# A long convolution stage and a transformer layer on one core: angles counted in turns, attention values with 512 moving columns, weights' low parts a window later in a third buffer

## The reference

```python
dt = jnp.exp(log_dt)
dt_Lambda = dt[:, None, 0] * Lambda[None, :, 0] + 1j * (dt[:, None, 1] * Lambda[None, :, 1])
...
Wc = Wc * num * _reciprocal(den * Lam, EPS)
P = dt_Lambda[..., None] * pos - P_max[..., None]
K = jnp.einsum('chn,hnl->chl', Wc, jnp.exp(P))
return K.real.astype(jnp.float32)
```

```python
attn = jax.nn.softmax(scores, axis=-1)
ctx = jnp.einsum('bhqk,bhkd->bhqd', attn, v_h)
ctx = ctx.transpose(0, 2, 1, 3).reshape(b, t, D_OUT)
return ctx @ Wo
...
h = _L0_tok_ref(L0_tok_log_dt, L0_tok_Lambda, x, 1024)
h = h + _L0_attn_ref(_layernorm(h, axis=-1), ...)
h = h + _L0_ffn_ref(_layernorm(h, axis=-1), ...)
```

## Time and profile before

| | us |
|---|---|
| median of 3 runs | 2391.71 (2391.33 to 2392.13) |
| the profiled execution, whole | 2390.53 |
| its span, first to last instruction | 2388.7 |
| one chunk of the first stage (122.44 to 149.07) | 26.63 |
| the layer stage's first instruction | 262.1 |

### The profile page before, as it was taken

One profiled execution on the slowest core, in us unless ns is written; L12 is line 12 of the kernel. 1 busy time (PEld: TensorE's weight loads), 2 busy tenths in 40 slices (PEclk: granted clock), 3 DMA queues, 4 the chain that ended last, 5 costly groups with the idle time before them and its releaser, 6 DMA issues.

```text
span 2388.7 us, 58825 instructions
## 1 busy us (share of the span) xinstructions
PE 2276.2 (95%) x18704; PEld 1246.2 (52%) x18704; DVE 1908.7 (80%) x7797; ACT 1836.2 (77%) x6269; POOL 1708.1 (72%) x1529
## 2 busy tenths in 40 slices
PE   2999689999999999999999999999999999999986
PEld 2777345555555555555555555555555555555543
DVE  8999578888788788888788878888888878888864
ACT  5998388777877777878777787777787777778773
POOL 1444187877777777777787777777777777777772
PEclk9999899999999999999999999999999999999997
DMA  2888599999999999999999999999999999999984
GB/s 77 263 252 240 135 172 186 187 186 191 189 185 194 188 183 193 191 187 185 191 184 190 192 190 186 189 193 177 192 191 187 187 193 190 180 196 186 184 170 100
DMA packets 1201602, 443.65 MB, mean 186 GB/s; under 512 B 1151622, under 2 KB 1153926, under 8 KB 1201292
## 3 DMA queue, kind: packets, MB, share of 16 engines
q1 hardware_dynamic: 1201284, 439.89, 91.5%
q10 hardware_dynamic: 8, 0.01, 0.0%
HBM read 87.40 MB, written 67.11 MB: 65 GB/s over the span
## 4 chain that ended last, share of the span: by engine, by line
PE 83%; ACT 2%; POOL 1%; DMA 1%; DVE 1%; issue 1%; POOLq 0%; DVEq 0%; ACTq 0%
PE pc L907 13%; PE pb L907 13%; PE pa L907 13%; PE s_ps L920 5%; PE pb L893 4%; PE pb L895 4%; PE pb L894 4%; PE pa L893 4%; PE pa L894 4%; PE pa L895 4%; PE pv_ps L935 4%; PE pd L893 2%; PE pd L895 1%; PE pd L894 1%; DMA pt<-p 1%; ACT pr L1059 1%
## 5 line engine op out<-in xcount | busy, mean ns | idle before, releaser
L1059 ACT ACTIVATE pr<-pr,smin 128x128 f32<-128x128 f32 x2048 | 793.5, 388 | 235.9 <-DVE smin L1205 235.7
L1425 POOL TENSOR_TENSOR pr<-pr,rinv 128x512 f32<-128x512 f32 x512 | 577.0, 1137 | 424.2 <-DVE rinv L1213 413.5
L1205 DVE CUSTOM_DVE_ANT_0 pr<-s_ps,cst 128x128 f32<-128x128 f32 x2048 | 468.7, 286 | 180.2 <-PE s_ps L920 95.7
L1433 POOL TENSOR_TENSOR p<-pr,p 128x512 f16<-128x512 f32 x512 | 590.1, 1158 | 23.9 <-ACT p L1069 13.0
L1069 ACT ACTIVATE p<-pr 128x512 f16<-128x512 f32 x512 | 319.0, 623 | 181.0 <-POOL pr L1425 153.4
L1059 ACT ACTIVATION_READ_ACCUMULATOR pr<-pr,smin 128x1 f32 x2048 | 382.1, 187 | 0.0
L907 PE MATMUL pa<-wkv_hi,xt 128*128 128x512 f16 x1024 | 326.3, 380 | 14.8 <-DMA xt<-xs 14.8
L907 PE MATMUL pb<-wq_hi,xt 128*128 128x512 f16 x1024 | 326.6, 380 | 0.0
L907 PE MATMUL pc<-wq_hi,xt 128*128 128x512 f16 x1024 | 315.0, 379 | 0.0
L642 PE MATMUL hps<-z,xw 128*128 128x256 f32 x848 | 193.7, 388 | 62.1 <-POOL xw L348 42.2
L642 PEld LDWEIGHTS hps<-z,xw 128*128 128x128 f32 x848 | 162.4, 194 | 92.9 <-POOL xw L348 50.5
(11 more groups left out here) (188 smaller groups left out, 4896.2 us busy)
## 6 DMA issues: line engine op xcount, KB each, us to landing
h<-rows SPq DMA_DIRECT2D x128, 256.0 KB, 3.5
h_res<-h SPq DMA_DIRECT2D x64, 512.0 KB, 4.5
out<-rows SPq DMA_DIRECT2D x64, 512.0 KB, 3.2
h_ln<-h SPq DMA_DIRECT2D x63, 512.0 KB, 4.2
pt<-p SPq DMA_TRANSPOSE x512, 3.8
xa<-x SPq DMA_DIRECT2D x16, 256.0 KB, 4.1
xb<-x SPq DMA_DIRECT2D x32, 128.0 KB, 3.8
wst<-wq SPq DMA_DIRECT2D x8, 512.0 KB, 5.7
```

What stands on the lines that cost most here:

```text
L1059: last = A.activation(p, p, ACT.Exp, bias=smin[g % 2][:, j:j + 1], scale=-1.0, accum_out=rsum[g % 2][:, j:j + 1])
L1205: V.tensor_tensor_reduce(pr[g % 2][:, cols], s_ps[g % 2][:, cols], mask, 1.0, 3e38, ALU.add, ALU.min, smin[g % 2][:, j:j + 1]).then_inc(ma ...
L1425: nc.gpsimd.tensor_tensor(p3, p3, rinv[g % 2][:, :].unsqueeze(2).broadcast_to([P, HG, P]), ALU.mult).then_inc(p_norm, 1)
L1433: nc.gpsimd.tensor_tensor(p[:, HG * P:], pr[g % 2][:, :], p[:, 0:HG * P], ALU.subtract).then_inc(pl_done, 1)
```

## The change

- Angles are counted in turns instead of radians: the rate `zi` is multiplied with 1/(2 pi) once at the start, and the whole turns are taken out with one pass of two operations (add a large number, subtract it) and one subtraction. The factor 2 pi goes into the sines' `scale`. `half` becomes twice the squared sine (`scale` of the square), so that `tables` is one pass, (half - 1) times expo, with the sign changed; `digits` is the same and the sign is taken up in the weights' last steps.
- `ON_ACT` is 3 in even windows and 2 in odd ones: in odd windows DVE makes two tokens of `xw` instead of one.
- `pi` has two buffers: DVE waits for the add two windows back instead of the one before.
- `wst` has three buffers, low parts are made one window later than in the list, and POOL's table steps no longer wait for low parts.
- `values` takes the four heads of a group as one moving operand of 512 columns, and four groups go to the four strips. The rows of `wo` are put into the matching order when inputs are laid out, before the kernel runs.

```diff
-ON_ACT = 3
+ON_ACT = (3, 2)
...
-                    if n >= 2:
-                        sp.wait_ge(w_lo, n - 1)
+                    if n >= WR:
+                        sp.wait_ge(w_lo, n - WR + 1)
...
-                    while loaded < len(PIECES) and PIECES[loaded - 2][0] <= w:
+                    while loaded < len(PIECES) and PIECES[loaded - WR][0] + LOW_LATER <= w + 1:
                         load_weight(loaded)
...
-                        lows = sum(piece[0] < w - 1 for piece in PIECES)
-                        if at in (0, 2, 3) and lows:
-                            pool.wait_ge(w_lo, lows)
...
-                    V.tensor_scalar(turns[:, :, :], theta[:, :, :], INV_2PI, MAGIC, ALU.mult, ALU.add).then_inc(tab_v, 1)
+                    V.tensor_scalar(turns[:, :, :], theta[:, :, :], MAGIC, MAGIC,
+                                    ALU.add, ALU.subtract).then_inc(tab_v, 1)
                     dve.wait_ge(tab_v, TV * k + 1)
-                    V.tensor_scalar(turns[:, :, :], turns[:, :, :], MAGIC, None, ALU.subtract).then_inc(tab_v, 1)
...
-                    V.tensor_scalar(theta[:, :, :], theta[:, :, :], PI_SAFE, -PI_SAFE,
-                                    ALU.min, ALU.max).then_inc(tab_v, 1)
+                    V.tensor_tensor(theta[:, :, :], theta[:, :, :], turns[:, :, :], ALU.subtract).then_inc(tab_v, 1)
...
-                    V.tensor_scalar(half[:, :, :], half[:, :, :], -2.0, 1.0, ALU.mult, ALU.add).then_inc(tab_v, 1)
...
-                    V.tensor_tensor(tab[k % 2][:, :, 0, :], expo[:, k * TC:k * TC + TC, :], half[:, :, :],
-                                    ALU.mult).then_inc(tab_v, 1)
+                    V.scalar_tensor_tensor(tab[k % 2][:, :, 0, :], half[:, :, :], 1.0,
+                                           expo[:, k * TC:k * TC + TC, :], ALU.subtract, ALU.mult).then_inc(tab_v, 1)
...
-                    if w >= 1:
-                        dve.wait_ge(xw_done, w)
+                    if w >= 2:
+                        dve.wait_ge(xw_done, w - 1)
...
                     for n, piece in enumerate(PIECES):
-                        if piece[0] == w:
+                        if piece[0] + LOW_LATER == w:
                             weight_lo(n)
+                weight_lo(len(PIECES) - 1)
...
-                        to = slice(P * (g % 4), P * (g % 4) + P)
-                        for n, (v, lo) in enumerate(((v_hi[odd], 0), (v_lo[odd], 0), (v_hi[odd], HG))):
-                            for j in range(HG):
-                                last = pe.matmul(pv_ps[j * HD:(j + 1) * HD, to], v[:, g * HD:(g + 1) * HD],
-                                                 pt[g % RP][:, lo + j, :], start=(n == 0), stop=(n == 2))
+                    for n, (v, lo) in enumerate(((v_hi[odd], 0), (v_lo[odd], 0), (v_hi[odd], HG))):
+                        for g in range(4 * m, 4 * m + 4):
+                            strip = slice(HD * (g % 4), HD * (g % 4) + HD)
+                            last = pe.matmul(pv_ps[strip, :], v[:, g * HD:(g + 1) * HD],
+                                             pt[g % RP][:, lo:lo + HG, :], start=(n == 0), stop=(n == 2))
```

More of the change, by code:

```diff
@@ L150, in s4_stage @@
         cst = W["cst"]
-        re_row, im_row, neg_re_row, row_sign = (cst[:, c:c + 1] for c in (C_RE, C_IM, C_NRE, C_SIGN))
+        re_row, im_row, row_sign = (cst[:, c:c + 1] for c in (C_RE, C_IM, C_SIGN))
         z = [sb(f"z{i}", [P, 4, QROW]) for i in range(ZR)]
@@ L156, in s4_stage @@
         xw = [sb(f"xw{i}", [P, WIN, TOPS, NB]) for i in range(XWR)]
-        pi = sb("pi", [P, WIN, TOPS, NB])
+        pi = [sb(f"pi{i}", [P, WIN, TOPS, NB]) for i in range(2)]
         expo = sb("expo", [P, T, NPOS])
@@ L162, in s4_stage @@
         hout = [W[f"rows{i}"] for i in range(HR)]
-        wst = [sb(f"wst{i}", [P, KC * AW]) for i in range(2)]
+        wst = [sb(f"wst{i}", [P, KC * AW]) for i in range(WR)]
         top_r = sb("top_r", [P, TOPS, T])
@@ L212, in s4_stage @@
         x_in = [sem(f"x_in{i}") for i in range(XR)]
-        w_in = [sem(f"w_in{i}") for i in range(2)]
+        w_in = [sem(f"w_in{i}") for i in range(WR)]
         w_hi = sem("w_hi")
@@ L244, in loads_until @@
         def loads_until(n):
-            return 16 * sum(PIECES[i][4] for i in range(n % 2, n + 1, 2))
+            return 16 * sum(PIECES[i][4] for i in range(n % WR, n + 1, WR))
         def weight(name, k):
@@ L375, in sines @@
                 def sines(k):
-                    act.wait_ge(tab_v, TV * k + 5)
-                    A.activation(half[:, :, :], theta[:, :, :], ACT.Sin, scale=0.5).then_inc(tab_a, 1)
+                    act.wait_ge(tab_v, TV * k + 2)
+                    A.activation(half[:, :, :], theta[:, :, :], ACT.Sin, scale=0.5 * TURN).then_inc(tab_a, 1)
                     act.wait_ge(tab_a, TA * k + 1)
-                    A.activation(theta[:, :, :], theta[:, :, :], ACT.Sin).then_inc(tab_a, 1)
-                    A.activation(half[:, :, :], half[:, :, :], ACT.Square).then_inc(tab_a, 1)
+                    A.activation(theta[:, :, :], theta[:, :, :], ACT.Sin, scale=TURN).then_inc(tab_a, 1)
+                    A.activation(half[:, :, :], half[:, :, :], ACT.Square, scale=ROOT_2).then_inc(tab_a, 1)
                 def products(w, e):
@@ L409, in _ @@
                 act.wait_ge(pre_v, V_F)
-                A.activation(sy, pf, ACT.Sin).then_inc(pre_a, 1)
-                A.activation(hy, pf, ACT.Sin, scale=0.5).then_inc(pre_a, 1)
+                A.activation(sy, pf, ACT.Sin, scale=TURN).then_inc(pre_a, 1)
+                A.activation(hy, pf, ACT.Sin, scale=0.5 * TURN).then_inc(pre_a, 1)
                 sines(0)
@@ L420, in _ @@
                 for w in range(LEAD):
-                    for e in range(ON_ACT):
+                    for e in range(ON_ACT[w % 2]):
                         products(w, e)
@@ L427, in _ @@
                     for e in range(WIN):
-                        if e < ON_ACT and w + LEAD < WINDOWS:
+                        if w + LEAD < WINDOWS and e < ON_ACT[(w + LEAD) % 2]:
                             products(w + LEAD, e)
@@ L551, in _ @@
                 step(V.tensor_tensor(yi, *lengthened(zi), ALU.mult))
-                step(V.tensor_scalar(pk, yi, INV_2PI, MAGIC, ALU.mult, ALU.add))
-                step(V.tensor_scalar(pk, pk, MAGIC, None, ALU.subtract))
-                step(V.scalar_tensor_tensor(pf, pk, -TWO_PI_HI, yi, ALU.mult, ALU.add))
-                step(V.scalar_tensor_tensor(pf, pk, -TWO_PI_LO, pf, ALU.mult, ALU.add))
-                step(V.tensor_scalar(pf, pf, PI_SAFE, -PI_SAFE, ALU.min, ALU.max))
+                step(V.tensor_scalar(pk, yi, MAGIC, MAGIC, ALU.add, ALU.subtract))
+                step(V.tensor_tensor(pf, yi, pk, ALU.subtract))
                 assert steps[0] == V_F
```

66 lines of the change are left out of this document (31 added, 35 removed).

## The result

The changed kernel takes 2370.78 us (median of 4 runs, 2369.04 to 2371.53), the one before 2391.52 us beside it on the same chip: 20.7 us less, a ratio of 0.9915 with a 95% interval of 0.9898 to 0.9932. The profiled execution took 2371.53, its span is 2369.1.

What follows compares the result with a forecast made beforehand. DVE was taken to bound the first stage (26.63 us a chunk, PE's floor 24.3), PE the layer stage. Gains of 15.3 and 1.7 us make 17: 2390.53 becomes 2374 profiled, 2375 median; range 2370 to 2380 (50%).

Steps and rivals of the forecast that it cites:

- The table pass, its place and its price: First stage, DVE's pass making `tab`: begins 14.38 us into the chunk, waits for POOL's late add, plus 2.1 us per chunk.
- The waits for ACT: First stage, DVE's two waits for ACT's high parts go when low parts come a window later: minus 1.54 us per chunk.
- The start: First stage ahead of the chunks: shorter angle passes and one table pass gone, minus 4.1 us in all.
- Chunk 0: First chunk: 1.2 us as the others, `pi` 0.4, and `wkv_lo` 0.6 moved into the next chunk: minus 2.2 us.
- Chunks 1 to 6: First stage, middle chunks: 25.4 us each instead of 26.63, minus 7.4 us together.
- Chunk 7: Last chunk: ACT wait of 1.63 us goes, `wo_lo` moves behind the last `z`, `wkv_lo` and longer `xw` enter: minus 1.6.
- POOL against the low parts: First stage: POOL's passes become free as DVE starts `wo_lo` and `wq_lo`; DVE wins, 0; otherwise plus 2.1 us per chunk.
- Rival 2: First stage: POOL's passes get in ahead of DVE's low parts, chunks of 27.5 us, 2387 us in all; 14%.
- SP's stores: First stage: h0 stores stand behind weight loads that wait 4 to 5 us; counted 0, at worst 1 us per chunk.
- Rival 1: First stage: DVE wins the race at `tab` and PE sets the pace, chunks of 24.3 us, 2367 us in all; 25%.
- The layer stage: Values step in three rounds of 512 columns, minus 2.7 us; waits for transposes at the end, plus 1: minus 1.7.
- rival 3: Values step: four strips do not stream together at 512 columns, about 2620 us (5%), or in part, 2396 us (3%).

Runs made afterwards that it cites:

- sines early: Changed kernel with ACT's sines for the next chunk moved from the start of a chunk's second window to its first window, behind the second eviction: 2356.84 us.
- add first: Changed kernel with POOL's order turned round in the window of `table_i`, the add ahead of `table_i`: 2364.96 us.
- three products: Changed kernel with three tokens of products on ACT in every window, `ON_ACT = (3, 3)`, as before the change: 2370.45 us.
- one `pi`: Changed kernel with one buffer of imaginary products instead of two: 2370.23 us.
- POOL's waits: Changed kernel with POOL's waits for the low parts of the weights put back: 2370.81 us.

## Why the prediction held, point by point

- **The table pass, its place and its price: right.** Forecast 14.38 us into the chunk, the sine's end 12.95, the add 14.3 to 16.65; measured 14.71 (14.37 in chunks 3 and 6), 12.95, and 14.27 to 16.63. The pass took 2.47 us, and the chunk 25.29 where 25.4 stood. That the meeting was the cause, and not DVE's sum, is shown by sines early and add first, which move work without taking any from DVE, and by three products, which takes 0.54 us from DVE and gains nothing. The changed kernel's own chunks say it too: where the second sine ends 12.95 or 12.96 us in (chunks 1, 3, 4 and 6), the chunk lasts 25.28 to 25.30, though chunk 1 has 1.28 us more of low parts; where it ends at 13.15 (chunk 2), 25.49, and at 13.86 (chunk 5), 26.03.
- **The waits for ACT: right that they go with late low parts**, and these carry most of the gain. The prediction took the angles' 1.64, the tables' 0.64 and the waits' 1.54 as one sum. As a sum it is right (23.35 for 23.37, with early sines), but its terms are not independent: without the late low parts the first two are worth nothing in a chunk.
- **The start: right**, PE's first matmul at 38.18 for 42.22, 4.04 us.
- **Chunk 0: too high, mostly by PE's clock.** Forecast 2.2 us, measured 0.5 (the sixth `pi` 69.16 to 64.62, less the 4.04). After 38 us without a matmul PE's records start 0.427 us apart, the rate of the lower clock level (1.2 GHz), and then 0.216; the rise came 6.0 us after the first matmul in this execution and 3.5 in the one before. The windows from 41 to 44 us of this kernel and of the one with one `pi`, where it came after 2.7 us (the clock column has no entry this early and prints 1.00):
```profile
41.00:44.00 3.00, 3.00 (x9) 2.37 (x8) 3.00 (x3) 1.54 (x5) 1.13 (x1) 1.00 0.00 0
```
```profile
41.00:44.00 3.00, 3.00 (x15) 2.65 (x14) 3.00 (x2) 2.15 (x6) 1.62 (x1) 1.00 0.00 0
```
Evictions wait for PE and the sines for evictions, hence DVE's 1.80 us. With one `pi` and with three products (3.0 us) chunk 0 gains 2.0 us by the same sum, as forecast, although the low part is as long there; with POOL's waits (5.7 us), 0.7. What set the moment is not shown.
- **Chunks 1 to 6: right**, 7.15 for 7.4 (228.97 to 217.28, less the 4.54 ahead). **Chunk 7: too low**, 2.98 for 1.6; 0.7 of it lies behind PE's last matmul, and no run takes it apart. The two misses cancel, by luck: 14.67 in all for 15.
- **POOL against the low parts: right**, DVE's low parts beside POOL's small passes are 1.21 to 1.22, and POOL's passes give way. (The two long `wq_lo`, 3.38 and 3.37 in chunks 0 and 5, wait for the add.) Rival 2 did not come.
- **SP's stores: counted 0, at worst 1 us per chunk; they cost about 0.9 in all.** SP stands up to 2.3 us before a load of weights (4 to 5 were forecast), and ACT's evictions wait 20.0 us for stores of h0. In most chunks that is over before the sines are due. In chunk 5 it is not: ACT waits 2.73 us, has two evictions to catch up, and makes the second sine 0.91 us later than in chunk 4; DVE's pass then comes ahead of the add, and the low part waits.
```profile
176.62 1.08 ACT L399 ACTIVATE rows<-hps 128x512 f32<-128x512 f32 x2 [2.73 <-DMA h<-rows]
...
179.20 0.63 ACT L378 ACTIVATE theta<-theta 128x512 f32<-128x512 f32 x1
...
179.91 1.27 POOL L265 TENSOR_TENSOR tab<-expo,theta 128x512 f32<-128x512 f32 x1 [4.03 <-ACT theta L378]
...
180.38 1.35 DVE L465 SCALAR_TENSOR_TENSOR tab<-turns,expo 128x512 f32<-128x512 f32 x1
...
181.14 2.80 POOL L350 TENSOR_TENSOR xw<-xw,pi 128x1024 f32<-128x1024 f32 x1
...
181.65 3.37 DVE L520 SCALAR_TENSOR_TENSOR wq_lo<-wst,wq_hi 128x1024 f16<-128x1024 f32 x1
```
Chunk 5 is 0.74 longer for it, and chunk 2, with a sine 0.20 late in the same way, 0.20. With early sines 4.7 us of these waits are left and PE is busy throughout, so they hold nothing there.
- **Rival 1: its floor was right, its price too low.** PE's 24.3 measures 24.17 with early sines, the nearest kernel to that case, which takes 2357 and not 2367. What the price left out lies at the ends, in PE's chunks 0 and 6 and behind them.
- **The layer stage: forecast 1.7, measured 4.9.** The values step gives 3.2 for 2.7 (0.85 us between its neighbours, 1178.60 to 1179.45, as forecast), and rival 3 is refuted: rounds of 512 columns start 0.22 us apart in the changed kernel. Its 18 us were also too many by its own reading: if twelve quads needed all of the 0.78, three rounds of 0.26 need the same 0.78. The ends were given 1 us of loss and show 1.7 of gain. But the layer stage from its first instruction to the end of the span is 2121.2 to 2123.9 us in ten kernels with the new values step (mean 2122.6) and 2123.9 to 2126.6 in four with the old one (mean 2125.7): 3.1 apart, which is the values step alone. The ends scatter by 2.6 us from kernel to kernel and are not shown to be the change's.
- **The whole: 2370.78 where 2375 stood**, near the lower end of 2370 to 2380. In the profiled execution (2371.53 for 2374) the first stage gained 0.3 us less than forecast and the layer stage 3.2 more, most of it at the ends. The mechanism held; that its sum came this close is in part luck.

## What to carry to other kernels

Where two engines hold each other up, an instruction's busy time can be a wait: look for one that is several times its own usual length, and for what the other engine runs over it. Work taken off an engine ahead of a wait for a third engine is worth nothing until that wait is gone, so find the last wait of the period first and place each edit ahead of it or behind it. The remedy lay on an engine that was not full (ACT, 21.48 us of a chunk of 25.29): its sines, up to 3.45 us earlier in the chunk (8.87 for 12.32 in the chunks shown), brought 14 us on top of the change's 21, since POOL stood behind ACT, and DVE behind POOL.

## What the hardware showed

- In these rows DVE and POOL on SBUF take turns by instruction, and whoever already waits goes next, ahead of what the other has queued. With the add first, DVE's pass waits and is served at the add's end, then `table_i`, and only then DVE's low part, whose 2.29 us hold 1.1 of waiting. With three products on ACT the order is `table_i`, pass, add, low part (3.37 us). The Trainium skill (SBUF — State Buffer, SBUF: two separate sides) says that the first to start keeps the port pair for its whole instruction; these rows agree, and add who is next.
- Four strips of 32 columns with 512 moving columns each run at the rate of one: rounds 0.22 us apart, where single matmuls of 512 columns start 0.216 apart at clock 1.00. The Trainium skill (TensorE: Matmul & The Clock Gate, Part 3: Packing small matmuls — row/col tiling) has 2.38 times for three; no run here has three, and for four this trace shows 3.9 times.
